# Causal attention in front of a mixture of experts: heads laid in strips of 32 array rows

## The reference

```python
xn = _layernorm(x)
# attention on xn
h = xn @ W1 + b1                      # (B, S, 3E), per head 8 q, 8 k, 8 v
w = einsum('bhqd,bhkd->bhqk', q, k) / sqrt(d)
w = softmax(w * tril - (1 - tril) * 1e6)
a = einsum('bhqk,bhkd->bhqd', w, v) -> (B, S, E);  attn = a @ Wp + bp
# experts on xn
shared = (silu(xn @ sg.T) * (xn @ su.T)) @ sd.T
probs = softmax(xn @ gate_w.T); two best, weights normalised
routed = sum of the two chosen experts' outputs, weighted
out = x + attn + shared + routed
```

## Time and profile before

| | |
|---|---|
| median of 3 runs | 681.55 us (680.13 to 684.37) |
| span of the profiled execution | 678.1 us, 14263 instructions |
| PE busy | 609.9 us (90%) |
| DVE, ACT, POOL busy | 469.8, 316.3, 311.2 us |
| mean granted PE clock | 0.981 |

### The profile page before, as it was taken

The page is one execution under the profiler, slowest core; times in us unless marked ns, Lnnn a source line. Parts: engine busy times, 40 slices in busy tenths (PEclk is TensorE's granted clock), DMA queues, the critical chain, the costliest instruction groups (busy, mean ns, idle before and its releaser), DMA issues.

```text
span 678.1 us, 14263 instructions
## 1 busy us (share of the span) xinstructions
PE 609.9 (90%) x4034; PEld 417.5 (62%) x4035; DVE 469.8 (69%) x981; ACT 316.3 (47%) x626; POOL 311.2 (46%) x361
## 2 busy tenths in 40 slices
PE   0368989999999999999999999889999999997984
PEld 0255645555555555455555554389999999975663
DVE  6957869878676776666676774755555555538987
ACT  0220455646555555455565656643333333354452
POOL 9500021214346455555646222526666554465563
PEclk9968999999999999999999999999999999999998
DMA  5070712472414425225135016012222222423454
GB/s 136 2 184 6 183 38 94 96 298 95 110 33 132 105 72 131 72 89 140 45 113 133 10 49 241 1 48 62 62 63 62 62 62 62 117 69 98 137 155 124
DMA packets 58204, 64.26 MB, mean 95 GB/s; under 512 B 6608, under 2 KB 40240, under 8 KB 57904
## 3 DMA queue, kind: packets, MB, share of 16 engines
q1 hardware_dynamic: 53808, 54.79, 28.8%
q0 software_dynamic: 4352, 8.95, 4.3%
HBM read 32.96 MB, written 30.48 MB: 94 GB/s over the span
## 4 chain that ended last, share of the span: by engine, by line
PE 66%; DVE 14%; DMA 8%; issue 5%; ACT 2%; SPq 2%; POOL 1%; DVEq 1%; ACTq 0%; POOLq 0%
PE bank L640 12%; PE bank L648 10%; PE bank L625 10%; PE bank L808 7%; PE bank L629 4%; DVE o_sb L1500 4%; PE bank L819 4%; PE bank L613 3%; DMA k_st<-k_rows 3%; DVE neg_max L1324 2%; PE bank L655 2%; PE bank L794 2%; DVE xn_rows L1210 2%; DMA out<-o_sb 2%; PE bank L798 2%
## 5 line engine op out<-in xcount | busy, mean ns | idle before, releaser
L1324 DVE TENSOR_REDUCE neg_max<-bank 128x1 f32<-128x384 f32 (+3 forms) x352 | 216.8, 638 | 102.2 <-PE bank L629 89.3
L1040 ACT ACTIVATE probs<-bank 128x512 f32<-128x512 f32 (+1 forms) x352 | 189.8, 562 | 158.2 <-PE bank L640 148.7
L515 POOL TENSOR_SCALAR_AFFINE_SELECT probs<-probs 128x512 f32<-128x512 f32 x128 | 86.0, 681 | 243.5 <-ACT probs L1040 242.5
L640 PE MATMUL bank<-q_bd,k_st 128*128 128x512 f32 (+1 forms) x352 | 167.1, 482 | 5.1 <-DMA q_bd<-m_row 2.5
L625 PE MATMUL bank<-k_st,q_bd 127*128 127x384 f32 (+3 forms) x512 | 147.0, 343 | 10.1 <-issue 6.3
L640 PEld LDWEIGHTS bank<-q_bd,k_st 128*128 128x128 f32 x352 | 66.8, 192 | 75.7 <-issue 72.4
L625 PEld LDWEIGHTS bank<-k_st,q_bd 127*128 127x128 f32 x512 | 90.7, 193 | 32.0 <-issue 14.7
L583 POOL DMA_INDIRECT y_tok<-y_sb,y_rows x72 | 70.1, 973 | 71.9 <-ACT y_sb L1105 56.9
L648 PE MATMUL bank<-probs,v 128*32 128x512 f32 (+3 forms) x1024 | 95.5, 444 | 2.6 <-POOL probs L515 2.6
L629 PE MATMUL bank<-mask_qk,ident_bf 128*128 128x128 bf16 (+2 forms) x352 | 90.6, 257 | 0.0
L549 POOL DMA_INDIRECT sorted_x<-xn_rows,slot_idx x64 | 62.7, 979 | 15.3 <-issue 15.0
(11 more groups left out here) (165 smaller groups left out, 923.2 us busy)
## 6 DMA issues: line engine op xcount, KB each, us to landing
q_bd<-q_rows SPq DMA_DIRECT2D x32, 192.0 KB
k_st<-k_rows SPq DMA_DIRECT2D x32, 192.0 KB
sorted_x<-zeros SPq DMA_DIRECT2D x8, 580.5 KB, 6.2
xg<-sorted_x SPq DMA_DIRECT2D x36, 129.0 KB
q_rows<-q_hi SPq DMA_DIRECT2D x16, 256.0 KB
k_rows<-k_hi SPq DMA_DIRECT2D x16, 256.0 KB
picked<-y_tok SPq DMA_DIRECT2D x16, 256.0 KB, 3.9
egu_lo<-in_e_gu SPq DMA_DIRECT2D x2, 1408.0 KB, 9.4
```

The lines of the kernel that those rows point to most:

```text
L515: pool.affine_select(out=diag, in_=diag, compare_op=ALU.is_ge, fill=0.0, base=0, pattern=[[0, HG // heads], [0, heads], [1, P]], channel_m ...
L640: pe.matmul(dst[:, 0:nh * w], k_st[par][:, g, kb * P:(kb + 1) * P], q_bd[par][:, h0:h0 + nh, kb * P:S], start=True, stop=True).then_inc(st ...
L1040: act.activation(probs[:, u, 0:w], src[:, 0:w], ACT.Exp, scale=SCALE).then_inc(exp_done[u], 1)
L1324: dve.tensor_reduce(neg_max[:, g, heads[0]:heads[0] + nh, qb], src[:, 0:nh * w].rearrange("p (h w) -> p h w", h=nh), AX.X, ALU.max, negate ...
```

## The change

- Each head keeps its own strip of 32 partitions for q as well as for k (`q_st`, `k_st`); nothing is block diagonal and no buffer is cleared. The rows of a strip are interleaved (4 rows per d: three parts and one spare), the columns of W1 are ordered so that each projected part goes from SBUF to SBUF by one DMA with partition stride 4 (`strips_in`), with three buffers for three batches. The spare rows are set once (`last_rows_in`): zeros, and a one in the row where the maxima go.
- A matmul for maxima or scores uses only the 31 or 32 rows of its head, so it occupies a row tile of the array; two heads of maxima and two heads of scores, in four strips and four PSUM banks, are issued one behind the other.
- Maxima come in 6 units per group, each of two heads in a pair of banks, reduced by one DVE instruction (two in the units of the shortest query blocks): 8 reductions for 11. Scores come in 12 units through a ring of three banks, which also serves all projections and transposed copies (`ST_NO`, `MX_NO` number the fills, two semaphores per ring).
- Everything is written out in 34 steps of one group (s = -2 to 31) that replace the batch bodies: step s has the maxima of group s+2, the scores of group s, the values of group s-1. Values use 9 columns per head where 32 were used.
- The start: x comes in 8 loads, the reciprocal root is an integer estimate with three Newton steps on DVE (it was a table root on ACT with one), done batch by batch; four batches are normalised in the start, the other four in steps -1 to 2, the router runs in two halves (steps -1 and 4), the routing in steps 5 to 13, the scatters in steps 14 to 29, four per step.
- Moves between engines: the split of q and k for batches 1 to 7 goes from ACT and DVE to ACT and POOL (`whole`, `split`), value rows from DVE to ACT with the v bias folded into the output bias (`bout2`), the feature copy from DVE to ACT. POOL masks in three instructions per group for four. The expert weights are loaded in steps 16 to 20 and split on DVE in and behind steps 30 and 31.
- The experts' and the output stage's own instructions stay, but for the bias `bout2` and buffer addresses.

```diff
-            def split_rows_out(b, par):
-            def split_rows_in(b, par):
+            def strips_in(b, c):
+                hi, lo, strip = ((q_hi, q_lo, q_st), (k_hi, k_lo, k_st))[c]
...
+                for r, part in enumerate((hi, hi, lo) if c == 0 else (hi, lo, hi)):
+                    sp.dma_start(strip[b % NBUF][r::4, :, :].bitcast(F32), part[:].bitcast(F32)).then_inc(qk_ld[b % NBUF], 16)
+            def max_row_in(n):
...
+                sp.dma_start(q_st[b % NBUF][31::32, g, :].bitcast(F32), m_row[g][:].bitcast(F32)).then_inc(m_ld[n % 2], 16)
...
-            for k in range(2):
-                ins = pool.memset(k_st[k][:].bitcast(F32), 0.0)
-            pool.memset(q_bd[0][:].bitcast(F32), 0.0).then_inc(cleared, 1)
-            pool.memset(q_bd[1][:].bitcast(F32), 0.0).then_inc(cleared, 1)
...
+            def max_scores(n, u):
+                if i >= 2:
+                    pe.wait_ge(mx_free, i - 1)
+                for c, (qb, lo) in enumerate(MX_PARTS[u // 2]):
+                    w = (qb + 1) * P
+                    for k in range(2):
+                        j = 2 * (u % 2) + k
+                        pe.matmul(mx_pair[i % 2][:, k, lo:lo + w], q_st[buf][32 * j:32 * j + 31, g, qb * P:(qb + 1) * P],
+                                  k_st[buf][32 * j:32 * j + 31, g, 0:w], start=(c == 0), stop=False, skip_group_check=True)
+            def max_masks(n, u):
+                for k in range(2):
+                    ins = pe.matmul(mx_pair[i % 2][:, k, lo:lo + blocks * P], ident_bf[:], mask_qk[:, 0:blocks, :],
+                                    start=False, stop=True, skip_group_check=True)
+            def scores(n, pair):
+                for u in pair:
+                    i = ST_NO["S", n, u]
+                    pe.wait_ge(st_free, i - 2)
+                for c, (kb, lo) in enumerate(parts):
+                    w = S - kb * P
+                    for u in pair:
+                        ins = pe.matmul(st_banks[:, i % 3, lo:lo + w], k_st[buf][32 * j:32 * j + 32, g, kb * P:(kb + 1) * P],
+                                        q_st[buf][32 * j:32 * j + 32, g, kb * P:S], start=(c == 0), stop=True, skip_group_check=True)
...
+            for s in range(-2, GROUPS):
+                maxima, scored, valued = s + 2 < GROUPS, s >= 0, s >= 1
+                if maxima:
+                    max_scores(s + 2, 0)
+                if scored:
+                    scores(s, (2, 3))
+                if maxima:
+                    max_masks(s + 2, 0)
+                if valued:
+                    values(s - 1, 0)
...
+                if s >= -1:
+                    turn(s)
+                if valued:
+                    values(s - 1, 1)
...
+                if valued:
+                    values(s - 1, 3)
+                    values(s - 1, 2)
...
+                if s % 4 == 2 and s <= 22:
+                    project((s + 6) // 4, 0)
...
+            def maxima(n, u):
+                dve.wait_ge(mx_full, i + 1)
+                for qb, lo in MX_PARTS[u // 2]:
+                    ins = dve.tensor_reduce(neg_max[:, g, h:h + 2, qb], mx_pair[i % 2][:, :, lo:lo + (qb + 1) * P], AX.X, ALU.max, negate=True)
+                ins.then_inc(mx_free, 1)
```

More of the change, by code:

```diff
@@ L24 @@
 NG = H // HG
+GROUPS = B * NG
 NX = 8
@@ L652, in to_tokens @@
[L652 to L661 removed]
             def x_transposes(b):
+                i = ST_NO["xT", b]
@@ new lines, in router @@
+            def router(half_of):
+                i = ST_NO["lg", half_of]
+                first = half_of * NT // 2
+                pe.wait_ge(gate_ld, 16)
+                pe.wait_ge(st_free, max(i - 2, used_up("xT", (half_of + 1) * EARLY - 1)))
+                for n in range(NT // 2):
+                    ins = pe.matmul(st_banks[:, i % 3, n * NX:(n + 1) * NX], xnT[:, (first + n) * P:(first + n + 1) * P], gate[:],
+                                    start=(n == 0), stop=True, skip_group_check=True)
+                ins.then_inc(st_full, 1)
@@ new lines, in turn @@
+            def turn(s):
+                i = MX_NO["T", s]
+                pe.wait_ge(mx_free, i - 1)
+                if s + 1 < GROUPS:
+                    pe.wait_ge(mx_free, reduced("M", s + 1, NMX - 1))
+                    ins = pe.transpose(mx_pair[i % 2][0:HG * NB, 0, 0:P], neg_max[:, (s + 1) % NG].rearrange("p h n -> p (h n)"), ident[:])
+                if s >= 2:
+                    pe.wait_ge(av_out, s - 1)
+                    for k in range(NB):
+                        ins = pe.transpose(mx_pair[i % 2][:, 1, k * P:(k + 1) * P], av_sb[s % 2][:, k * P:(k + 1) * P], ident[:])
+                ins.then_inc(mx_full, 1)
@@ L922, in _ @@
-            for b in range(2):
-                attention(b, b, True, True)
-            with pe.Fori(1, B // 2 - 1) as i:
-                for par in range(2):
-                    attention(("r", i), par, True, True)
-            attention(B - 2, 0, True, False)
-            attention(B - 1, 1, False, False)
-            pe.wait_ge(aT_ready, B + PRIME_ATOUT)
+            values(GROUPS - 1, 0)
+            turn(GROUPS)
+            values(GROUPS - 1, 1)
+            values(GROUPS - 1, 3)
+            pe.wait_ge(st_free, ST_ALL)
@@ new lines, in _ @@
+            pe.wait_ge(columns_set, 2)
+            x_step(0, 0)
+            values(GROUPS - 1, 2)
+            pe.wait_ge(mx_free, MX_ALL)
+            pe.wait_ge(egu_split, NX)
+            gate_up(0, load_columns(0), 1)
+            pe.wait_ge(av_out, GROUPS)
+            for k in range(NB):
+                ins = pe.transpose(bank[5][:, k * P:(k + 1) * P], av_sb[(GROUPS - 1) % 2][:, k * P:(k + 1) * P], ident[:])
+            ins.then_inc(t_last, 1)
+            pe.wait_ge(a_last, 1)
+            for k in range(NB):
+                ins = pe.transpose(bank[6][:, k * P:(k + 1) * P], a_tok[:, k, :], ident[:])
@@ new lines, in results_out_of @@
+            def results_out_of(n):
+                act.wait_ge(av_full, n + 1)
+                if n >= 2:
+                    act.wait_ge(mx_full, reduced("T", n))
+                act.activation(av_sb[n % 2][:], av_bank[:], ACT.Copy).then_inc(av_out, 1)
+            act.wait_ge(consts, 1)
+            act.activation(primed[:, 3:4], ident[:, 0:1], ACT.Exp)
+            x_out_of(0)
+            act.wait_ge(w_ld, 32)
+            first_high(0)
+            first_high(1)
+            for b in range(1, EARLY):
+                x_out_of(b)
@@ new lines, in _ @@
+            first_low(0)
+            first_low(1)
+            normal_rows(2)
+            normal_rows(3)
+            for s in range(-2, GROUPS - 2):
+                maxima(s + 2, 0)
+                maxima(s + 2, 1)
+                if s >= -1:
+                    turned(s)
+                maxima(s + 2, 2)
+                maxima(s + 2, 3)
+                if -1 <= s < B - EARLY - 1:
+                    normal_rows(s + EARLY + 1)
+                if s == 5:
+                    route_exponents()
+                if s == 6:
+                    route_probabilities()
+                    route_best(0)
+                if s == 7:
+                    route_choice(0)
+                    route_best(1)
+                if s == 8:
+                    route_choice(1)
+                    route_chosen()
+                if s == 9:
+                    route_weights()
+                if s == 11:
+                    route_blocks()
+                    route_rows()
+                if s == 12:
+                    route_tiles()
+                maxima(s + 2, 4)
+                maxima(s + 2, 5)
@@ L1361, in x_low @@
+            turned(GROUPS - 2)
+            for x in range(4):
+                split_weights(x)
+            turned(GROUPS - 1)
+            for x in range(4, NX):
+                split_weights(x)
+            turned(GROUPS)
             def x_low(t, par):
```

1137 lines of the change are left out of this document (508 added, 629 removed).

## The result

| | us | against the kernel before, 95% interval |
|---|---|---|
| before, median of 3 | 681.55 | |
| changed, median of 3 | 664.77 (659.67 to 670.04) | 0.9719 (0.9648 to 0.979) |
| the same changed kernel, measured again (run e17), median of 4 | 636.67 (634.67 to 638.68) | 0.9313 (0.9261 to 0.9365) |
| forecast | 592 (560 to 646) | 0.869 |

Ratios and their intervals use fast executions alone: the slowest of the first measurement (670.0) and one of the kernel before beside e17 (941.8, at a clock of 0.568) were slow. The first measurement is 73 us above the forecast and outside its range. The same program, measured a second time on another occasion, took 28 us less, 45 above the forecast and inside the range, while the median of the kernel before hardly moved (684.0 beside e17).

The account below looks back on a forecast made before the run. PE was taken as the bound (busy 46.5 of 47.0 us a batch), its step falling from 11.7 to 9.1 us. Start, steps and an experts' stage of 235.9 gave 588.4, plus 3.45 made 592 us, range 560 to 646.

Parts of the forecast that it names:

- median above span: Whole kernel: the median of before lay 3.45 us above its profiled span, and the same was added to 588.4.
- the step: Steady step on PE: strips, masks, tile changes, values, turn, projections and features sum to 8.6, plus 0.5 waits: 9.1 us for 11.7.
- changes of tile: PE's switches between row strips and whole array in a steady step: 15 at 0.135 us, 2.0 us.
- A: Steady steps: weight loads of row strips run one after the other, 1.8 us more a step, 641 us; chance 0.11.
- B: Steady steps: each tile change costs the pipeline's whole latency, 0.27 us, 2.0 more a step, 646 us; chance 0.12.
- C: Steady steps: strips do not overlap at all, 3.3 us more a step, 681 us; chance 0.05.
- the start's order: Start: normalising four batches on DVE sets the first reduction, at 25.4 us; the projection way ends at about 22.
- rival D: Steady steps: the clock falls to 1.2 GHz, 5.4 us more a step, 737 us; chance 0.02 with other slower ends.
- 5 for routing bursts: Steps 5 to 12: 5 us added to 8 x 9.1 for routing on DVE between the fourth and fifth unit.
- what was moved to ACT and POOL is hidden by PE's 9.1: Steady step: work moved to ACT and POOL costs nothing; without that cover 0.4 and 1.0 us a step.
- DVE 6.8 + 4.5 = 11.3 each: Steps 0 to 2: DVE's usual 6.8 us plus 4.5 for one batch's normal rows, 11.3 us a step, to 77.3.

Follow-up runs that it names:

- e17: The changed kernel measured once more on another occasion, nothing altered: 636.67 us (0.9313).
- e4: The changed kernel with DVE's normal rows of batches 4 to 7 and the seven routing bundles cut into pieces behind each maxima unit: 619.1 us (0.907).
- e18: Unaltered repeat of e4 plus maxima twice in the start, every fourth step and the end, and last scores twice: 626.2 us (0.9185).
- e10: The changed kernel with only the routing calculation cut into pieces behind each maxima unit, normal rows left whole: 623.5 us (0.9141).

## Why the prediction failed, step by step

Against e17, by the forecast's own milestones (a copy lies about two thirds into its step; that is an estimate from the timeline):

| stage | forecast | e17 | |
|---|---|---|---|
| to copy 1 | 62.2 | 71.55 | +9.3 |
| copy 1 to 3 (normal rows) | 21.2 | 31.2 | +10.0 |
| copy 3 to 5 (second router half) | 24.2 | 23.7 | -0.5 |
| copy 5 to 13 (routing) | 77.8 | 93.1 | +15.3 |
| copy 13 to 29 | 145.6 | 149.9 | +4.3 |
| to the first gate_up | 21.5 | 28.9 | +7.4 |
| experts and output | 235.9 | 238.5 | +2.6 |
| median above span | 3.45 | -0.1 | -3.6 |

That is 45 us, 637 for 592. The runs show by experiment the 12 to 15 us of the routing and 5 of the 10 of the normal rows; for the other rows the cause is argued from the traces.

- **Right: the step.** 9.0 to 9.4 for 9.1, with strips abreast, changes of tile at (228.01 - 227.79 - 2 x 0.053) = 0.11 for 0.135 in e17, and DVE at 6.95 for 6.8. ACT had 6.7 for 6.1, POOL 8.0 where 9.4 was the most. Rivals A, B and C are out by the starts at 227.26, 227.27 and 227.71: loads are not serial, a change does not cost 0.27. The four strips take 0.45 - 0.11 = 0.34 us, for 0.32 forecast. By the 3.07 times of the Trainium skill, "TensorE: Matmul & The Clock Gate", Part 3, it would be 0.28, an estimate; the trace agrees in kind and is 0.06 longer.
- **Right: the start's order.** First reduction at 27.0 for 25.4.
- **Wrong: rival D, priced as all or nothing.** "PE has hardly a pause in a step, so I give it little" looked at the steady step alone. The clock was at 1.2 GHz in the start, in and behind the bundles, and at the end: from e17's windows, 44.55 x 0.92 = 41 us before copy 1, 15 to copy 3, 24 in steps 5 to 12, 17 at the end, and 18 in the 16 steady steps. The row that warned of it was there: 0.79 at the start and 0.83 with PE busy 6.3 of 10. I took the maxima of the start and steps 30 and 31 at full clock (6.5 us each; at a clock of 0.62 and 0.54 they took 11.2 and 9.2). So the term for the clock was put at nothing where e17 has some 122 us at 1.2 GHz between the first reduction and the first gate_up; what that time cost is not known as a whole.
- **Wrong: "5 for routing bursts".** The bundles came to 12 to 15 us. I took them as DVE's busy time in a step with 9.1 - 6.8 = 2.3 us to spare. But a bundle stands in the queue in front of the fifth unit, PE is only two units ahead, and what PE loses by waiting it does not get back, since PE itself is the bound (8.9 of 9.0 us); and it goes on at half clock. The 2.3 us to spare were also too many while POOL's instructions ran beside the bundle: "what was moved to ACT and POOL is hidden by PE's 9.1" left out that POOL's work makes DVE's longer, by 3.9 us over the routing (17.9 for 14.0).
- **Wrong: "DVE 6.8 + 4.5 = 11.3 each" for steps 0 to 2.** The same mistake: steps 1 and 2 took 14.9 and 16.2. In pieces (e4) they took 12.8 and 13.8.
- **Not in any step: the occasion.** 28 us of the first measurement's 73 are gone in e17. In the traces they lie in steps 13 to 28, the steps with scatters, where PE's results came late. Its cause is open, and so is why the kernel before was spared: it has the same 64 scatters, and PE was its bound too, busy 46.5 of 47.0 us of a steady batch.

How much of the 45 us is the clock and how much is waiting was not separated as a whole: the runs that raised the clock did so by adding work. Bundles cut up gave 17 us back together with 32 to 34 us less at the low clock. The mean clock alone does not tell the time: e18 took 626.11 us at 0.920 and 626.19 at 0.942, which makes 100 and 72 us at 1.2 GHz, and e17 634.67 at 0.894 and 638.18 at 0.912.

## What to carry to other kernels

When a change makes PE the bound of every step, look up what still stands in one piece on the other engines' queues: a bundle costs its length beyond PE's lead (0.3 to 0.9 us here), not its share of the step, and cutting it behind each unit got back 17 us of 637 here. Take its length from a trace in which the other engines run beside it. Price the clock per stage, from the stages in which PE waits, and not from the steady one. And measure the changed kernel twice on different occasions before explaining a loss: one occasion made 28 us here, and with them a wrong theory that two runs seemed to show.

## What was not expected of the hardware

- Results of PE came 0.75 to 1.40 us behind the recorded ends in 9 of 18 steps of one execution, in step 14 at a recorded clock of 1.00, and in none of another of the same program; only steps with POOL's scatters had it. Whole medians moved with it, 664.8 to 636.7 and 657.3 to 626.2, while those of the kernel before lay between 681.6 and 684.0.
- A DVE scan of 128 x 32 elements took 0.21 to 0.22 us with POOL idle (e10) and up to 1.30 beside a POOL instruction, ending 0.08 us after it (e17, step 11).
- The clock fell to 1.2 GHz in steps in which PE is busy 9.5 of 9.9 us by the records: in e17 in each fourth step from 16 on, in e10, with the same instructions there, in none before copy 27. One such step cost 1.35 us.
